# Row maxima from two 64-row array tiles, one maximum over two PSUM banks, and a transpose for the turn

## What is computed

```python
x = x + conv(_gn(x))          # _gn: normalise over groups of 32 tokens
# inside conv, for every batch b and head h:
q, k, v = xs @ Wq, xs @ Wk, xs @ Wv
scores = einsum('bhtd,bhsd->bhts', q, k) * 64 ** -0.5
att = softmax(scores, axis=-1)
out = einsum('bhts,bhsd->bhtd', att, v)
out = out @ Wproj + bproj
```

## Time and profile before

| | |
|---|---|
| median of three runs | 4951.76 us (4950.67 to 4953.74) |
| profiled execution, span from first to last instruction | 4946.9 us |
| TensorE matmuls (PE) | 4705.1 us busy, 95%, 20608 |
| VectorE (DVE) | 2775.5 us, 56% |
| ScalarE (ACT) | 2886.6 us, 58% |
| GpSimd (POOL) | 2326.6 us, 47% |
| mean granted TensorE clock | 0.994 of full |

### The profile page before, as it was taken

One profiled execution on the slowest core, in us unless ns is written; L12 is line 12 of the kernel. 1 busy time (PEld: TensorE's weight loads), 2 busy tenths in 40 slices (PEclk: granted clock), 3 DMA queues, 4 the chain that ended last, 5 costly groups with the idle time before them and its releaser, 6 DMA issues.

```text
span 4946.9 us, 73065 instructions
## 1 busy us (share of the span) xinstructions
PE 4705.1 (95%) x20608; PEld 3505.4 (71%) x20608; DVE 2775.5 (56%) x5284; ACT 2886.6 (58%) x5507; POOL 2326.6 (47%) x1837
## 2 busy tenths in 40 slices
PE   7999999999999999999999999999999999999998
PEld 5777767777676776767767677676776767767675
DVE  5655646556465564655646556465564655646454
ACT  4665646556465564655646566464664646656465
POOL 2444545445454454544545445454444545445455
PEclk9999999999999999999999999999999999999999
DMA  2111111111111111111111111211112111111101
GB/s 69 34 37 55 31 53 35 46 46 32 52 34 50 43 34 54 31 53 41 32 54 35 51 41 30 63 28 53 37 30 62 35 49 35 32 61 34 53 23 51
DMA packets 156934, 212.71 MB, mean 43 GB/s; under 512 B 56544, under 2 KB 57568, under 8 KB 156512
## 3 DMA queue, kind: packets, MB, share of 16 engines
q1 hardware_dynamic: 156512, 207.47, 15.0%
HBM read 105.12 MB, written 34.08 MB: 28 GB/s over the span
## 4 chain that ended last, share of the span: by engine, by line
issue 50%; POOL 42%; PE 6%; POOLq 1%; ACT 1%; DVE 0%; DMA 0%; SPq 0%; ACTq 0%; DVEq 0%
POOL prob_l L1031 32%; POOL o L1048 6%; POOL res L1054 3%; PE bank L517 1%; PE bank L561 1%; POOLq L1030 1%; POOL rstd L1023 1%; PE bank L578 1%; PE bank L690 1%; PE bank L692 1%; PE bank L691 1%; PE bank L571 0%; PE bank L572 0%; POOLq L1047 0%; DMA xs<-in_x 0%
## 5 line engine op out<-in xcount | busy, mean ns | idle before, releaser
L1031 POOL TENSOR_TENSOR prob_l<-prob,prob_h 128x512 fp32r<-128x512 f32 x1408 | 1803.5, 1288 | 2470.5 <-ACT prob_h L710 2452.6
L710 ACT ACTIVATE prob<-bank 128x512 f32<-128x512 f32 x2048 | 1237.6, 604 | 1698.6 <-PE bank L572 1579.3
L864 DVE TENSOR_REDUCE smax<-bank 128x1 f32<-128x512 f32 x2048 | 1349.1, 684 | 1012.6 <-PE bank L578 997.8
L710 ACT ACTIVATE prob_h<-bank 128x512 fp32r<-128x512 f32 x2048 | 1236.7, 604 | 198.6 <-PE bank L692 154.9
L690 PE MATMUL bank<-prob_h,vh 128*128 128x512 f32 x2048 | 832.6, 407 | 117.9 <-ACT acc L781 99.3
L578 PE MATMUL bank<-k_hl,q_hh 128*128 128x512 f32 x2048 | 802.5, 436 | 33.6 <-DVE smax L864 30.4
L571 PE MATMUL bank<-q_hh,k_hl 128*128 128x512 f32 x2048 | 824.0, 402 | 0.5 <-ACT prob_h L710 0.5
L572 PE MATMUL bank<-q_lm,k_h 65*128 65x512 f32 x2048 | 813.8, 397 | 0.0
L692 PE MATMUL bank<-prob_l,vh 128*128 128x512 f32 x2048 | 809.6, 395 | 0.0
L691 PE MATMUL bank<-prob_h,vl 128*128 128x512 f32 x2048 | 809.0, 395 | 0.0
L803 DVE TENSOR_TENSOR prob_l<-prob,prob_h 128x512 fp32r<-128x512 f32 x640 | 508.0, 804 | 511.9 <-ACT prob_h L710 511.8
(11 more groups left out here) (58 smaller groups left out, 4393.2 us busy)
## 6 DMA issues: line engine op xcount, KB each, us to landing
xs<-in_x SPq DMA_DIRECT2D x128, 256.0 KB, 2.8
q_hh<-q_hh SPq DMA_DIRECT2D x256, 128.0 KB, 2.2
k_hl<-k_h SPq DMA_DIRECT2D x256, 128.0 KB, 2.4
inv_b<-inv_dram SPq DMA_DIRECT2D x256, 128.0 KB, 2.8
res<-in_x SPq DMA_DIRECT2D x128, 256.0 KB, 2.7
out_x<-res SPq DMA_DIRECT2D x128, 256.0 KB, 2.0
q_lm<-q_lm SPq DMA_DIRECT2D x256, 2.0 KB
den<-acc SPq DMA_DIRECT2D x256, 2.0 KB, 1.7
```

Source lines behind the costliest of these rows:

```text
L710: return nc.scalar.activation(out, ps[ST + bank][:, :], ACT.Exp, scale=SCALE)
L864: nc.vector.tensor_reduce(smax[:, j:j + 1], ps[SM + j % 2][:, :], AX.X, ALU.max).then_inc(rows_used, 1)
L1031: nc.gpsimd.tensor_tensor(prob_l[:, r3, :], prob[:, ring2, :], prob_h[:, r3, :].bitcast(F32), ALU.subtract).then_inc(prob_l_pool, 1)
```

## The change

The row scores use k-high alone: q-high times k-high needs 64 rows of contraction. The two halves of the keys become two matmuls of 64 rows, one on array rows 0 to 63 and one on rows 64 to 127, each into its own bank. One VectorE instruction takes the negated maximum over both banks, 1024 columns, straight into `nmax`; `smax`, `combine` and the semaphore `nmax_ready` go. Both banks are now freed together, so TensorE waits for the maximum just before. The key tensor is `k_lh` instead of `k_hl`: k-low on partitions 0 to 63 and k-high on 64 to 127; the copy by DMA now goes from `k_lh` to `k_h1`, of the same size. The turn of the maxima is a transpose, as `xt` is, in place of a matmul with the identity. The tables `MAXIMA` now count pairs, eight a step.

```diff
 MAXIMA = {
-    "plain": (0, 0, 2, 1, 1, 1, 2, 0, 1, 2, 1, 2, 1, 1, 1, 0),
+    "plain": (0, 0, 1, 0, 1, 0, 1, 0, 1, 1, 1, 1, 0, 1, 0, 0),
...
-    "tokens": (0, 1, 1, 1, 1, 1, 1, 1, 1, 2, 1, 2, 1, 2, 0, 0),
+    "tokens": (0, 0, 1, 0, 1, 0, 1, 1, 1, 1, 0, 1, 0, 1, 0, 0),
...
                 elif kind == "mt":
-                    nc.tensor.matmul(w[0:4, 0:P], nmax[:, a * 4:(a + 1) * 4], ident[:, :],
-                                     start=True, stop=True).then_inc(mt_done, 1)
+                    nc.tensor.transpose(w[0:4, 0:P], nmax[:, a * 4:(a + 1) * 4], ident[:, :]).then_inc(mt_done, 1)
...
-            def row_scores(slot, j):
-
-                t, half = divmod(j, 2)
-                nc.tensor.matmul(ps[SM + j % 2][:, :], q_hh[:, slot, t * P:(t + 1) * P],
-                                 k_hl[:, slot, half * 512:(half + 1) * 512], start=True, stop=True).then_inc(rows_ready, 1)
+            def row_scores(slot, t):
+
+                queries = slice(t * P, (t + 1) * P)
+                nc.tensor.matmul(ps[SM][:, :], q_hh[0:D, slot, queries], k_h1[0:D, slot, 0:512],
+                                 start=True, stop=True)
+                nc.tensor.matmul(ps[SM + 1][:, :], q_hh[D:P, slot, queries], k_lh[D:P, slot, 512:T],
+                                 start=True, stop=True).then_inc(rows_ready, 1)
...
-                            pe.wait_ge(nmax_ready, s.heads(2, 0 if a else 1, 2 if a else 1))
+                            pe.wait_ge(rows_used, s.heads(TT, 0 if a else 1, 8 if a else 4))
...
-                    pe.wait_ge(rows_used, s.heads(BLOCKS, 1, j - 1))
+                    pe.wait_ge(rows_used, s.heads(TT, 1, j))
                     row_scores((s.k + 1) % 2, j)
...
-                    nc.vector.tensor_tensor(k_hl[D:P, slot, cols], w[D:P, :], k_h1[0:D, slot, cols].bitcast(F32),
+                    nc.vector.tensor_tensor(k_lh[0:D, slot, cols], w[D:P, :], k_lh[D:P, slot, cols].bitcast(F32),
                                             ALU.subtract).then_inc(k_split, 1)
...
-            def take_max(j, count):
+            def take_max(t, count):
                 dve.wait_ge(rows_ready, count)
-                nc.vector.tensor_reduce(smax[:, j:j + 1], ps[SM + j % 2][:, :], AX.X, ALU.max).then_inc(rows_used, 1)
-
-            def combine(half, used):
-
-                dve.wait_ge(rows_used, used)
-                nc.vector.tensor_reduce(nmax[:, 4 * half:4 * half + 4],
-                                        smax[:, 8 * half:8 * half + 8].rearrange("p (t a) -> p t a", a=2),
-                                        AX.X, ALU.max, negate=True).then_inc(nmax_ready, 1)
+                nc.vector.tensor_reduce(nmax[:, t:t + 1], row_banks[:, :, :].rearrange("p a k -> p (a k)"),
+                                        AX.X, ALU.max, negate=True).then_inc(rows_used, 1)
```

More of the change, by code:

```diff
@@ L70 @@
 MAXIMA = {
-    "plain": (0, 0, 2, 1, 1, 1, 2, 0, 1, 2, 1, 2, 1, 1, 1, 0),
-    "values": (0, 0, 2, 1, 2, 0, 2, 0, 1, 1, 2, 2, 1, 0, 2, 0),
-    "norm": (0, 2, 0, 1, 1, 1, 2, 1, 0, 1, 1, 2, 1, 1, 2, 0),
-    "tokens": (0, 1, 1, 1, 1, 1, 1, 1, 1, 2, 1, 2, 1, 2, 0, 0),
-    "next": (0, 0, 0, 0, 0, 0, 0, 2, 2, 2, 2, 2, 2, 2, 2, 0),
-    "proj": (0, 1, 1, 1, 2, 0, 1, 2, 1, 2, 1, 1, 1, 1, 1, 0),
+    "plain": (0, 0, 1, 0, 1, 0, 1, 0, 1, 1, 1, 1, 0, 1, 0, 0),
+    "values": (0, 0, 1, 0, 1, 0, 1, 0, 1, 1, 1, 1, 0, 1, 0, 0),
+    "norm": (0, 1, 0, 1, 1, 0, 1, 0, 0, 1, 1, 1, 0, 1, 0, 0),
+    "tokens": (0, 0, 1, 0, 1, 0, 1, 1, 1, 1, 0, 1, 0, 1, 0, 0),
+    "next": (0, 0, 0, 0, 0, 0, 0, 1, 1, 1, 1, 1, 1, 1, 1, 0),
+    "proj": (0, 1, 0, 1, 1, 0, 1, 1, 1, 1, 0, 1, 0, 0, 0, 0),
 }
@@ L266, in attention_block @@
         q_lm = sb("q_lm", [P, 2, T], F32R)
-        k_hl = sb("k_hl", [P, 2, T], F32R)
+        k_lh = sb("k_lh", [P, 2, T], F32R)
         k_h1 = sb("k_h1", [P, 2, T], F32R)
@@ L290, in attention_block @@
         minus_half = sb("minus_half", [P, 4])
-        ps = [ctx.enter_context(nc.psum_tensor(f"bank{n}", [P, 512], F32)) for n in range(8)]
+        ps = [ctx.enter_context(nc.psum_tensor(f"bank{n}", [P, 512], F32)) for n in range(ST + 3)]
+        row_banks = ctx.enter_context(nc.psum_tensor("row_banks", [P, 2, 512], F32))
+        ps += [row_banks[:, n, :] for n in range(2)]
+        ps += [ctx.enter_context(nc.psum_tensor(f"bank{n}", [P, 512], F32)) for n in range(SM + 2, 8)]
         weights_in = sem("weights_in")
@@ L426, in twice @@
                              q_hh[0:D, slot, cols].bitcast(F32)).then_inc(qk_twice[slot][a], 16)
[L427 to L428 removed]
+                sp.dma_start(k_h1[0:D, slot, cols].bitcast(F32),
+                             k_lh[D:P, slot, cols].bitcast(F32)).then_inc(qk_twice[slot][a], 16)
             twice(0, 0, 1)
@@ L570, in scores @@
                 s_bank = ps[ST + n_bank]
-                nc.tensor.matmul(s_bank[:, :], k_hl[:, slot, keys], q_hh[:, slot, queries], start=True, stop=False)
+                nc.tensor.matmul(s_bank[:, :], k_lh[:, slot, keys], q_hh[:, slot, queries], start=True, stop=False)
                 nc.tensor.matmul(s_bank[:, :], k_h1[0:D + 1, slot, keys], q_lm[0:D + 1, slot, queries],
                                  start=False, stop=True).then_inc(scores_ready, 1)
-            def row_scores(slot, j):
-                t, half = divmod(j, 2)
-                nc.tensor.matmul(ps[SM + j % 2][:, :], q_hh[:, slot, t * P:(t + 1) * P],
-                                 k_hl[:, slot, half * 512:(half + 1) * 512], start=True, stop=True).then_inc(rows_ready, 1)
+            def row_scores(slot, t):
[4 more added lines that the diff above has]
+                                 start=True, stop=True).then_inc(rows_ready, 1)
             nothing = lambda: None
@@ L610, in _ @@
                 pe.wait_ge(qk_twice[0][tc], 32)
[L611 to L616, removed]
+            for t in range(TT):
+                if t:
+                    pe.wait_ge(rows_used, t)
+                row_scores(0, t)
+                if t == 4:
+                    start_entry("mt", 0, wait=lambda: pe.wait_ge(rows_used, 4))
             start_entry("v", 2)
@@ L722, in take @@
                     nc.scalar.copy(q_hh[0:D, slot, cols], w[0:D, :])
-                    nc.scalar.copy(k_h1[0:D, slot, cols], w[D:P, :]).then_inc(qk_hi, 1)
+                    nc.scalar.copy(k_lh[D:P, slot, cols], w[D:P, :]).then_inc(qk_hi, 1)
                 if kind == "v":
@@ L907, in _ @@
                     take_rows(0, bk, 1)
-                    for j in range(10, BLOCKS):
-                        take_max(j, j + 1)
-                    combine(1, BLOCKS)
+                    for t in range(5, TT):
+                        take_max(t, t + 1)
                 else:
@@ L914, in _ @@
                 if (kind, a) == ("v", 1):
[L915 to L918, removed]
+                    for t in range(5):
+                        take_max(t, t + 1)
             for n in range(AHEAD):
```

6 lines of the change are left out of this document (1 added, 5 removed).

## The result

The changed kernel takes 5131.25 us (5130.49 to 5132.14), against 4951.22 us before in the same runs: the ratio is 1.0364, 95% interval 1.0349 to 1.0379. It is 180 us slower. The forecast was 5096 us, range 4750 to 5200.

What follows compares the result with a forecast made beforehand. TensorE, busy 95% of the span, was taken as the bound. Terms of -102, +266, +20 and -40 gave +144 us on the 4946.9 us span, thus 5091; with 4.9 us from span to median, 5096 us, range 4750 to 5200.

Steps and rivals of the forecast that it cites:

- Term 1: Turn of the maxima: as a transpose on the full array it costs 0.11 us, not 0.51; 102 us saved.
- Term 2: Row scores: a pair of 64-row matmuls costs 0.72 us with array switches, against 0.46 before; 266 us added.
- the lower bound of 0.61: Row scores: a pair's cost in us if both tiles' weight loads run side by side; 154 us added.
- Term 3: VectorE's maxima and the banks: both banks held until a 1.22 us maximum ends, so TensorE waits; 20 us added net.
- Term 4: TensorE's waits for ScalarE and others: longer pairs give those engines time; 40 us taken off.
- A: Row scores: 64-row tiles cause no drain, so the kernel gets faster, 4704 to 4817 us, likeliest 4760; chance 24%.
- B: Row scores: array drained but loads still brought forward, pair 0.41 to 0.52 us, time 4820 to 4930; chance 9%.
- C: Row scores: the two tiles do not run together, 389 us added there, about 5220 us; chance 6%.

Runs made afterwards that it cites:

- before_wide_turn: Kernel before, with the turn of the maxima still a two-pass fp32 matmul but 128 weight columns in place of 4: 4900.76 us, ratio 0.9900.
- same_tile: Changed kernel with both matmuls of a pair on array rows 0 to 63: 5294.89 us, ratio 1.0694.

## Why the prediction was right, and where not

*What bounds it.* Right: all that moved the time did so through TensorE, and VectorE's 121 us less brought nothing.

*Term 1, 102 us saved.* Right in mechanism and size: 0.11 us for the turn as read from L549, and 94 us of time. That the gaps hang on the 4 columns, only inferred in the prediction, is shown by before_wide_turn. The reason given, that 4 columns set L557 apart, is half of it: the transpose keeps its 4 columns and has no gaps.

*Term 2, 266 us added.* The mechanism is right: a pair of 64 rows among matmuls of 128 is a change of arrangement both ways, with empty array and open loads. Two sizes were off. The loads of the two tiles start together, so the pair costs 0.64 and not 0.72: the lower bound of 0.61 was nearer, 184 us by the trace. And in time the tiles cost 59 to 86 us in four comparisons, since drains and open loads cover waits for the banks that full pairs would have. By the Trainium skill's "TensorE: Matmul & The Clock Gate", Measured speedup vs the span model, each further tile that runs along adds some 4 ns. The trace agrees for the pair itself: the second matmul record starts 2 to 5 ns behind the first, in the pair shown both at 2127.20. That figure alone would have made the change a gain; the switch into the tiles and out of them, which L557 had shown, decided against it.

*Term 3, 20 us added.* This is the step that failed: 192 us stand in its place. The maximum's 1.22 us and the release were right. Wrong was the count of places: I took VectorE to be ready whenever a pair was, and named a `prob_l` ahead of the maximum without giving it a price. With eight matmuls between blocks 8 and 9 the count had no wait there, but the maximum starts 1.8 us behind the pair. At the place that was counted, blocks 10 to 11, full rows come 0.32 us late as computed and tiled ones only 0.03 beyond the drain. Two banks used in turn had left 30 us of idle time. How the 192 us divide between the shared banks, the long maximum and the tables I did not isolate: maxima of half the length take 77 of them back, other tables 85 (106 with tiles); how far these two overlap, no run shows.

*Term 4, 40 us given back.* It did not come: the idle time ahead of the values is 124 us for 118, and TensorE's as a whole grew from 242 to 363.

The errors of terms 2 and 3 had opposite signs: 266 where the tiles cost 80 in time, 20 where the rest cost 192. They share a cause in part, waits and switches that cover each other, but nothing in the working made them cancel. That +144 forecast came so near to the +180 measured is luck, and in part the direction is too: the transpose's 94 and the tiles' 80 nearly cancel, so with the 20 us of term 3 the change would have come out about even. It is the 192 us that the prediction did not see that make it slower. Rivals A, B and C are out: the array is drained, the loads are open, the tiles stream together. No run shows what a tiled pair costs in time where nothing waits for a bank; by the starts it is the 0.17 to 0.18 us above.

## What to carry to other kernels

Count a change of array tiling as an operation of its own: here some 0.4 us a pair in drains and open loads, to save one stream of 0.23. Before two buffers are released by one instruction, look at what stands ahead of that instruction on its engine at each place, not only at its duration. Of a change with several parts, run the parts: the one-line transpose alone gave 94 us, and the rest cost 272, nearly three times that.

## What was not expected of the hardware

Two 64-row tiles load their weights at the same time: both load records start at 2127.20. On one tile (same_tile) the second load starts 0.11 us behind the first. The granted clock can be part of a wait's price: behind the first long wait of the tokens step it is at 0.50 for 6.6 us, and tables that only move waits took the mean from 0.985 to 0.973. Not every wait does it: from 626 to 932 us the clock is at 1.00, though two values steps there wait 1.18 us ahead of block 9. What separates the two was not tested.
